# Batch norm and GELU with four slots for x, GELU ahead of the copies, and a quarter of the sums on TensorE

## The chip, the cores and the metric

The kernel runs on one NeuronCore of a Trainium2 chip. Five engines work side by side and meet only through semaphores: TensorE (PE, with its weight loads as PEld), VectorE (DVE), ScalarE (ACT), GpSimd (POOL) and SyncE (SP, which here issues DMAs). The metric is the device time of one execution in microseconds (us), smaller is better.

## The reference, cut to what matters

The input x is 8 images of 384 channels and 32 x 32 pixels, float32. The program computes

```
x = x + gelu(batch_norm(deform_conv(group_norm(x))))      # offsets and masks from two small convolutions
t = to_tokens(x)                                          # 8 x 1024 tokens of 384 channels
t = t + block_attention(layer_norm(t))
t = t + head_attention(layer_norm(t))
x = from_tokens(t)
```

The part around the change is the end of the first line. Batch norm needs mean and variance of each channel over all images, so it starts when the last convolution tile is done. `yn = (y - mean) * rsqrt(var + 1e-5) * gamma + beta`, then the exact GELU, then the sum with the input, the transposition from channels to tokens, and for each token mean and variance over its 384 channels, which the next layer norm uses.

## The kernel before, in words

The program is a row of blocks, and each block gives every engine its own instruction list. A barrier of all engines stands between two blocks. The first block makes the offsets and a table of corners, `deform_conv` gathers, mixes and multiplies (until 1567 us), `batch_norm_gelu` is the stage of this case (until 1671 us), `block_attention` and `head_attention` follow.

`batch_norm_gelu` works on halves of an image: a half is 4 tiles (GROUP) of 128 pixels, with 384 channels as 3 x 128 (CH). There are 16 halves, numbered 0 to 15 here. The tensor `y` holds the convolution's output of all images on chip, and later the tokens. In a turn on one half

- SP loads the half of x into `c_x` (L780, 768 KB). There are two slots, one for each half of an image, and a slot is loaded again when TensorE has transposed all of it (`transposed`);
- ACT applies scale, shift and GELU, one instruction for each of 3 channel blocks, into `c_act`, two slots (L860);
- POOL adds the two in place in `c_x` (L803), and a root for 4 tiles of the image before follows (L797, a power of -1/2 on 4 elements);
- TensorE transposes the sum, 12 transpositions for a half, three to a PSUM bank `c_tps`, four banks for a half (L895);
- ACT copies the first two banks into `y` (L872, `copies`), DVE copies the other two (L821) and takes their statistics (L822), then those of ACT's two from `y` (L829), and makes mean and variance of them (L832, L835, L836). `measured` and `copied` tell TensorE that the banks are free.

The order on each engine is written by hand. The first image's halves stand ahead of a loop on the chip (`Fori`) over the other seven images; ACT's loop runs GELU of a half, then the copies of the half before. DVE starts the stage with the statistics of batch norm (L844), for which it waits until `gamma` and `beta` have come (`consts`, L782 and L783, the first DMAs of the block).

In the listing below, `halves` is the helper that makes the first image and the loop.

Of the kernel before, what the change touches and what calls it, by code (L numbers as in the profile page):

```python
# [8 lines left out]
ACT = mybir.ActivationFunctionType  # L9
# [81 lines left out]
def build(nc, io):  # L91
# [6 lines left out]
    with ExitStack() as whole:  # L98
# [27 lines left out]
        with ExitStack() as layers:  # L126
            y = sb(layers, "y", [BLOCKS, CH, P])
            conv_stats = sb(layers, "conv_stats", [CH, GROUPS, 6])
            with ExitStack() as conv:
                tap_index = nc.dram_tensor("tap_index", (GROUPS, P, TAPS * GROUP), U32, kind="Internal").ap()  # L130
                corner_w = nc.dram_tensor("corner_w", (GROUPS, P, CORNERS * TAPS * GROUP), F32, kind="Internal").ap()
                w_conv = sb(conv, "b_w", [TAPS, CH, C])
                b_conv = sb(conv, "b_b", [CH])
                conv_consts = sem("conv_consts")
                offsets_and_table(nc, io, sem, sb, bank, x_img, table, ident, tap_index, corner_w, neg_half, y, w_conv,
                                  b_conv, conv_consts, shared)
                deform_conv(nc, io, sem, sb, bank, table, ident, tap_index, corner_w, y, conv_stats, w_conv, b_conv,
                            conv_consts, shared)
            with ExitStack() as blocks:
                w_qkv = sb(blocks, "d_w_qkv", [CH, 3 * C])  # L140
                w_proj = sb(blocks, "d_w_proj", [CH, C])
                rot_a = sb(blocks, "d_rot_a", [C])
                rot_b = sb(blocks, "d_rot_b", [C])
                w_ln = sb(blocks, "d_w_ln", [2, C])
                causal = sb(blocks, "d_causal", [P])
                block_consts = ((w_qkv, "w_qkv"), (w_proj, "w_proj"), (rot_a, "rot_cos"), (rot_b, "rot_sin"),
                                (w_ln, "w_ln"), (causal, "causal"))
                consts = sem("d_consts")
                batch_norm_gelu(nc, io, sem, sb, bank, x_img, ident, neg_half, y, conv_stats, token_stats, token_rstd,
                                block_consts, consts)  # L150
                block_attention(nc, io, sem, sb, bank, ident, neg_half, y, tokens, token_stats, token_rstd,
                                [tile for tile, _ in block_consts], consts, head_consts, b_quarters, head_loaded)
# [375 lines left out]
def deform_conv(nc, io, sem, sb, bank, table, ident, tap_index, corner_w, y, conv_stats, w_conv, b_conv, conv_consts, shared):  # L528
# [6 lines left out]
    with ExitStack() as mem:  # L535
# [21 lines left out]
        with nc.Block() as block:  # L557
            @block.sync
            def _(sp):
# [8 lines left out]
                for g in range(2):  # L568
                    load_places(0, g)
                with sp.Fori(0, BATCH - 1) as n:  # L570
# [159 lines left out]
def batch_norm_gelu(nc, io, sem, sb, bank, x_img, ident, neg_half, y, conv_stats, token_stats, token_rstd,  # L730
                    block_consts, block_loaded):

    WIDE = GROUP * P
    with ExitStack() as mem:
        x_in = [sb(mem, f"c_x{u}", [CH, WIDE]) for u in range(2)]
        act_out = [sb(mem, f"c_act{u}", [CH, WIDE]) for u in range(2)]
        gamma = sb(mem, "c_gamma", [CH])
        beta = sb(mem, "c_beta", [CH])
# [10 lines left out]
        consts = sem("c_consts")  # L749
        x_loaded = [sem(f"c_x_loaded{u}") for u in range(2)]  # L750
# [13 lines left out]
        LAST = BATCH - 1  # L764

        def halves(eng, turn):

            for u in range(2):
                turn(0, u, True)
            with eng.Fori(1, BATCH) as n:  # L770
                for u in range(2):
                    turn(n, u, False)

        with nc.Block() as block:
            @block.sync
            def _(sp):
                def turn(n, u, first):
                    if not first:
                        sp.wait_ge(transposed, GROUP * (2 * n + u - 1))
                    sp.dma_start(x_in[u][:], x_img[n, :, :, u * WIDE:(u + 1) * WIDE]).then_inc(x_loaded[u], 16)  # L780

                sp.dma_start(gamma[:], io["gamma"]).then_inc(consts, 16)  # L782
                sp.dma_start(beta[:], io["beta"]).then_inc(consts, 16)  # L783
                for u in range(2):
                    turn(0, u, True)
                for tile, name in block_consts:
                    sp.dma_start(tile[:], io[name]).then_inc(block_loaded, 16)
                with sp.Fori(1, BATCH) as n:
                    for u in range(2):
                        turn(n, u, False)  # L790

            @block.gpsimd
            def _(pool):
                def root(n, u):
                    group = bass.ds(TILES * n + GROUP * u, GROUP)
                    pool.wait_ge(token_var, 2 * n + u + 1)
                    nc.gpsimd.tensor_tensor(token_rstd[:, group], tvar[:, group], neg_half[:, 0:GROUP],  # L797
                                            ALU.pow).then_inc(token_done, 1)

                def turn(n, u, first):  # L800
                    pool.wait_ge(act_ready, 2 * n + u + 1)
                    pool.wait_ge(x_loaded[u], 16 * (n + 1))
                    nc.gpsimd.tensor_tensor(x_in[u][:], x_in[u][:], act_out[u][:], ALU.add).then_inc(summed, 1)  # L803
                    if not first:
                        root(n - 1, u)
# [3 lines left out]
                halves(pool, turn)  # L809
                for u in range(2):  # L810
                    root(LAST, u)

            @block.vector
            def _(dve):
                def turn(n, u, first):
                    c = Chain(dve, lchain, 3 * (2 * n + u))
                    for i in range(GROUP // 2, GROUP):
                        count = TILES * n + u * GROUP + i
                        dve.wait_ge(transposed, count + 1)
                        tile = tps[u * GROUP + i][:, 0:C]  # L820
                        nc.vector.tensor_copy(y[:, bass.ds(count, 1)].rearrange("p n o q -> p (n o q)"), tile)  # L821
                        last = nc.vector.bn_stats(tst[:, i], tile)  # L822
                    c.step(last)
                    dve.sem_inc(measured, 1)
                    dve.wait_ge(copied, 2 * n + u + 3)
                    dve.nop(nofuse=True)
                    for i in range(GROUP // 2):
                        tile = y[:, bass.ds(TILES * n + u * GROUP + i, 1)].rearrange("p n o q -> p (n o q)")
                        last = nc.vector.bn_stats(tst[:, i], tile)  # L829
# [4 lines left out]
                    group = bass.ds(TILES * n + u * GROUP, GROUP)  # L834
# [3 lines left out]
                dve.sem_inc(summed, 2)  # L838
                dve.sem_inc(measured, 2)
                dve.sem_inc(copied, 2)  # L840
                dve.wait_ge(consts, 32)
# [4 lines left out]
                nc.vector.tensor_scalar(var[:], mv[:, :, 1], 1e-5, None, ALU.add).then_inc(var_ready, 1)  # L846
                dve.wait_ge(rstd_ready, 1)
# [3 lines left out]
                halves(dve, turn)  # L851

            @block.scalar
            def _(act):
                def gelu(n, u):

                    act.wait_ge(summed, 2 * n + u + 1)
                    act.nop(nofuse=True)
                    for o in range(CH):
                        last = nc.scalar.activation(  # L860
                            act_out[u][:, o].rearrange("p (b q) -> p b q", q=P),
                            y[:, bass.ds(TILES * n + u * GROUP, GROUP), o], ACT.Gelu,
# [3 lines left out]
                def copies(n, u):  # L866

                    for i in range(GROUP // 2):
                        count = TILES * n + u * GROUP + i
                        act.wait_ge(transposed, count + 1)  # L870
                        act.nop(nofuse=True)
                        last = nc.scalar.activation(y[:, bass.ds(count, 1)].rearrange("p n o q -> p (n o q)"),  # L872
                                                    tps[u * GROUP + i][:, 0:C], ACT.Copy)
                    last.then_inc(copied, 1)

                act.wait_ge(coef_ready, 1)
                gelu(0, 0)
                gelu(0, 1)
                copies(0, 0)
                with act.Fori(1, BATCH) as n:  # L880
                    gelu(n, 0)
                    copies(n - 1, 1)
                    gelu(n, 1)
                    copies(n, 0)
                copies(LAST, 1)

            @block.tensor
            def _(pe):
                def turn(n, u, first):
                    pe.wait_ge(summed, 2 * n + u + 3)  # L890
                    pe.wait_ge(measured, 2 * n + u + 1)
                    pe.wait_ge(copied, 2 * n + u + 1)
                    for i in range(GROUP):
                        for o in range(CH):
                            last = nc.tensor.transpose(tps[u * GROUP + i][:, o * P:(o + 1) * P],  # L895
                                                       x_in[u][:, o, i * P:(i + 1) * P], ident[:])
                        last.then_inc(transposed, 1)

                halves(pe, turn)

# [1560 lines left out]
```

## Time and profile before

| | |
|---|---|
| median of 3 runs | 3674.73 us (3672.86 to 3677.05) |
| the profiled execution | 3672.31 us, of which the span from first to last instruction is 3670.5 us |
| the batch norm stage in it | about 1567 to 1671 us of the span |
| mean granted TensorE clock | 0.955 of full speed over the span |

Busy shares over the whole span (PE 91%, DVE 74%, ACT 61%, POOL 40%) average over all stages. The stage of this case is under 3% of the span, so it is read in windows of its own: what each engine does in one image, which wait ends last before it, and how long one turn of each engine takes where it does not wait.

### The profile page before, as it was taken

Reading aid. Unit: us, or ns where it says so; the run is one execution under the profiler, and the core shown is the slowest. Engines: PE = TensorE matmul, PEld = TensorE weight load, DVE = VectorE, ACT = ScalarE, POOL = GpSimd, SP = SyncE. Lnnn points to the kernel's source line nnn. Section 1 sums busy time; section 2 is a strip of 40 time slices with the busy share of each in tenths; the row PEclk is TensorE's granted clock in tenths of the full one; section 3 lists DMA queues with packets and bytes.
Section 4 is the critical chain, followed back from the end, with each engine's and each line's share of the span. In section 5 each row is a group of like instructions: output and inputs, shape, how many; then the busy total and the mean of one; then the engine's idle time right before and its main releaser. Section 6 shows DMA issues by size and latency. Waiting matters only on the chain. (4 is left out here: it accounts for less than half of the span.)

```text
span 3670.5 us, 62059 instructions
## 1 busy us (share of the span) xinstructions
PE 3327.3 (91%) x18046; PEld 1920.4 (52%) x18046; DVE 2721.3 (74%) x5169; ACT 2249.4 (61%) x5369; POOL 1453.6 (40%) x1544
## 2 busy tenths in 40 slices
PE   7969999999999999937999999977988889889897
PEld 3434444444444444436888888853444444444443
DVE  4468878888888888756888888855677776776765
ACT  3434444444444444455777777755977778787785
POOL 2134444444444444363222222221154454544635
PEclk9989999999999999968999999978999999999997
DMA  9999989888999899641000000011322232232221
GB/s 363 370 357 343 336 334 350 325 328 333 348 342 345 334 342 344 257 156 54 17 15 17 17 17 17 17 54 49 87 72 62 81 91 66 76 92 64 57 67 54
DMA packets 230540, 647.07 MB, mean 176 GB/s; under 512 B 31143, under 2 KB 127943, under 8 KB 229959
## 3 DMA queue, kind: packets, MB, share of 16 engines
q0 software_dynamic: 82944, 453.02, 32.9%
q1 hardware_dynamic: 147398, 191.91, 16.5%
q8 instruction: 64, 1.05, 0.1%
q14 instruction: 134, 1.09, 0.1%
HBM read 520.21 MB, written 79.18 MB: 163 GB/s over the span
## 5 line engine op out<-in xcount | busy, mean ns | idle before, releaser
L697 PE MATMUL b_acc<-b_sampled,b_w 128*128 128x512 f32 x2592 | 1210.7, 594 | 0.0
L632 DVE SCALAR_TENSOR_TENSOR b_mix<-shared,b_weight,b_mix 128x384 f32<-128x384 f32 x864 | 531.5, 621 | 139.7 <-ACT b_mix L655 83.3
L697 PEld LDWEIGHTS b_acc<-b_sampled,b_w 128*128 128x128 f32 x2592 | 449.2, 191 | 347.3 <-issue 347.3
L664 ACT ACTIVATE b_sampled<-b_tps 128x384 f32<-128x384 f32 x576 | 282.1, 490 | 567.7 <-PE b_tps L715 567.7
L1985 DVE TENSOR_REDUCE e_neg_top<-e_next 128x1 f32<-128x1024 f32 x384 | 469.5, 1223 | 191.8 <-PE e_next L2298 164.0
L632 DVE SCALAR_TENSOR_TENSOR b_mix<-b_got,b_weight,b_mix 128x384 f32<-128x384 f32 x864 | 530.6, 619 | 92.8 <-ACT b_mix L655 56.2
L2152 ACT ACTIVATE e_prob<-e_s 128x512 f32<-128x512 f32 x768 | 416.3, 598 | 128.0 <-PE e_s L2310 126.7
L2137 ACT ACTIVATE e_unused<-e_next,e_neg_top 128x1024 bf16<-128x1024 f32 x384 | 430.2, 1120 | 100.1 <-DVE e_neg_top L1985 100.1
L588 POOL DMA_INDIRECT shared<-corner_table,b_index x288 | 294.1, 1021 | 418.7 <-DVE b_mix L632 324.9
L588 POOL DMA_INDIRECT b_got<-corner_table,b_index x288 | 292.1, 1014 | 356.8 <-DVE b_mix L632 299.4
L715 PEld LDWEIGHTS b_tps<-ident,b_mix 128*128 128x128 f32 x1728 | 223.0, 142 | 370.7 <-issue 327.5
L1205 ACT ACTIVATE d_w_qkv<-d_back,d_neg_top 128x128 f32<-128x128 f32 x768 | 269.0, 389 | 136.0 <-DVE d_neg_top L1108 136.0
L715 PE MATMUL b_tps<-ident,b_mix 128*128 128x128 f32 x1728 | 287.3, 276 | 56.0 <-DVE b_mix L632 50.6
L2298 PE MATMUL e_next<-e_stack 96*128 96x512 f32 x768 | 299.4, 472 | 11.8 <-ACT e_unused L2137 6.9
L2310 PE MATMUL e_s<-e_stack 98*128 98x512 f32 x768 | 271.2, 425 | 6.1 <-ACT e_prob L2152 5.1
L655 ACT ACTIVATE b_mix<-shared,b_weight 128x384 f32<-128x384 f32 x288 | 177.2, 615 | 104.7 <-ACT b_sampled L664 54.6
L2324 PE MATMUL e_acc<-e_prob,e_v 128*32 128x512 f32 x1536 | 214.0, 630 | 7.1 <-DVE e_ctx L1999 5.8
L655 ACT ACTIVATE b_mix<-b_got,b_weight 128x384 f32<-128x384 f32 x288 | 177.1, 615 | 54.5 <-ACT b_sampled L664 51.0
L1035 POOL TENSOR_TENSOR d_rqk<-d_ms,neg_half 128x2 f32<-128x2 f32 x64 | 44.8, 700 | 411.8 <-DVE d_ms L1078 411.8
L2298 PEld LDWEIGHTS e_next<-e_stack 96*128 96x128 f32 x768 | 126.6, 196 | 145.4 <-issue 89.9
L2310 PEld LDWEIGHTS e_s<-e_stack 98*128 98x128 f32 x768 | 147.1, 196 | 67.8 <-ACT e_prob L2152 38.8
L1205 ACT ACTIVATION_READ_ACCUMULATOR d_w_qkv<-d_back,d_neg_top 128x1 f32 x768 | 176.2, 229 | 0.0
(225 smaller groups left out, 5362.7 us busy)
## 6 DMA issues: line engine op xcount, KB each, us to landing
corner_table<-y SPq DMA_DIRECT2D x32, 1536.0 KB, 14.8
e_stack<-e_high SPq DMA_DIRECT2D x384, 64.0 KB, 2.0
shared<-in_x SPq DMA_DIRECT2D x8, 1536.0 KB, 10.1
c_x<-in_x SPq DMA_DIRECT2D x16, 768.0 KB, 4.4
tokens<-y SPq DMA_DIRECT2D x64, 192.0 KB, 1.9
e_tok<-tokens SPq DMA_DIRECT2D x8, 1536.0 KB, 7.2
e_stack<-e_low SPq DMA_DIRECT2D x192, 64.0 KB, 2.0
shared<-tokens SPq DMA_DIRECT2D x8, 1536.0 KB, 7.3
```

Source lines behind the costliest of these rows:

```text
L588: nc.gpsimd.indirect_dma_start(out=got[t % SLOTS][:], out_offset=None, in_=table[:, :], in_offset=bass.IndirectOffsetOnAxis(ap=index[g][:, ...
L632: ins = nc.vector.scalar_tensor_tensor(dst[:], src[:, q * C:(q + 1) * C], weight[g][:, q, k, i:i + 1], dst[:], ALU.mult, ALU.add)
L655: nc.scalar.activation(mix[t % MIXES][:], got[t % SLOTS][:, 0:C], ACT.Copy, scale=weight[g][:, 0, k, i:i + 1]).then_inc(begun, 1)
L664: nc.scalar.activation(sampled[s % 2][:, :, i * P:(i + 1) * P], tps[t % 2][:, 0:C].rearrange("p (o q) -> p o q", q=P), ACT.Copy).then_inc( ...
L697: last = nc.tensor.matmul(acc[g][co][:], w_conv[:, k, ci, co * P:(co + 1) * P], sampled[s % 2][:, ci], start=(k == 0 and ci == 0), stop=(k ...
L715: last = nc.tensor.transpose(tps[t % 2][:, o * P:(o + 1) * P], mix[t % MIXES][:, o * P:(o + 1) * P], ident[:])
L1205: last = nc.scalar.activation(prob[:, head], b_s[r][:, c * P:(c + 1) * P], ACT.Exp, bias=neg_top[:, head:head + 1], scale=SCALE, accum_out ...
L1985: nc.vector.reduce_max(neg_top[s % 2][:, t:t + 1], b_next[t % 2][:], AX.X, negate=True).then_inc(top_ready, 1)
L2137: nc.scalar.activation(unused[t % 2][:], b_next[t % 2][:], ACT.Exp, bias=neg_top[s % 2][:, t:t + 1], accum_out=den[s % 2][:, t:t + 1]).the ...
L2152: nc.scalar.activation(prob[(2 * c + f) % 8][:], b_s[f][:], ACT.Exp).then_inc(prob_ready, 1)
L2298: last = nc.tensor.matmul(b_next[t % 2][:, f * HALF:(f + 1) * HALF], stack[k][0:96, 0, t * P:(t + 1) * P], stack[k][0:96, 1, f * HALF:(f + ...
L2310: nc.tensor.matmul(b_s[f][:], stack[k][0:98, 1, c * P:(c + 1) * P], stack[k][0:98, 0, f * HALF:(f + 1) * HALF], start=True, stop=True).the ...
```

## The change

In `batch_norm_gelu`:

- x has four slots in `shared` (memory that the convolution has used until then), one for each of four halves in a row, and a slot waits for the transpositions of four halves before. The six constants of the next block are loaded one by one behind the x loads of halves 4 to 9, where they stood ahead of the loop.
- `gamma` and `beta` are loaded at the start of `deform_conv`, and DVE waits for them only where it multiplies by gamma.
- ACT begins with a one-element GELU (`c_warm`). GELU of half h+2 stands ahead of the copies of half h; it waits for POOL's sum of h and for TensorE's first tile of h, both of which read the slot of `c_act`.
- POOL adds 3 of a half's 4 tiles. The last tile of the half goes first through TensorE: for each channel block a product of x with the identity and one of `c_act` with the identity, summed in PSUM, so 6 matmuls for that tile and 9 transpositions for the others.
- POOL's root is taken once an image, on 8 elements.
- All loops on the chip are written out, for 16 halves on each engine.

```
+            gamma = sb(layers, "c_gamma", [CH])
+            beta = sb(layers, "c_beta", [CH])
+            norm_loaded = sem("c_norm_loaded")
...
                 for g in range(2):
                     load_places(0, g)
+                sp.dma_start(gamma[:], io["gamma"]).then_inc(norm_loaded, 16)
+                sp.dma_start(beta[:], io["beta"]).then_inc(norm_loaded, 16)
...
-        x_in = [sb(mem, f"c_x{u}", [CH, WIDE]) for u in range(2)]
+        x_in = [shared[:, s].rearrange("p (o q) -> p o q", q=WIDE) for s in range(SLOTS)]
...
+        def tile_of(i):
+            return (i + GROUP - 1) % GROUP
...
+                def load_x(h):
+                    n, u = divmod(h, 2)
+                    if h >= SLOTS:
+                        sp.wait_ge(transposed, GROUP * (h - SLOTS + 1))
+                    sp.dma_start(x_in[h % SLOTS], x_img[n, :, :, u * WIDE:(u + 1) * WIDE]).then_inc(
+                        x_loaded[h % SLOTS], 16)
+                for h in range(SLOTS):
+                    load_x(h)
+                for h in range(SLOTS, HALVES):
+                    load_x(h)
+                    if h - SLOTS < len(block_consts):
+                        tile, name = block_consts[h - SLOTS]
+                        sp.dma_start(tile[:], io[name]).then_inc(block_loaded, 16)
...
+                for h in range(HALVES):
+                    pool.wait_ge(act_ready, h + 1)
+                    pool.wait_ge(x_loaded[h % SLOTS], 16 * (h // SLOTS + 1))
+                    x_part = x_in[h % SLOTS][:, :, 0:WIDE - P]
+                    nc.gpsimd.tensor_tensor(x_part, x_part, act_out[h % 2][:, :, 0:WIDE - P], ALU.add).then_inc(summed, 1)
+                    if h > 2 and h % 2:
+                        root(h // 2 - 1)
+                root(BATCH - 1)
...
-                dve.wait_ge(consts, 32)
                 c = Chain(dve, chain, 0)
...
+                dve.wait_ge(norm_loaded, 32)
                 dve.wait_ge(rstd_ready, 1)
...
+                nc.scalar.activation(warm[:], neg_half[:, 0:1], ACT.Gelu)
                 act.wait_ge(coef_ready, 1)
...
+                for h in range(2):
+                    gelu(h)
+                for h in range(HALVES):
+                    if h + 2 < HALVES:
+                        gelu(h + 2)
+                    copies(h)
...
+                for h in range(HALVES):
+                    slot = x_in[h % SLOTS]
+                    if h >= 2:
+                        pe.wait_ge(measured, h - 1)
+                        pe.wait_ge(copied, h - 1)
+                    pe.wait_ge(x_loaded[h % SLOTS], 16 * (h // SLOTS + 1))
+                    pe.wait_ge(act_ready, h + 1)
                     for i in range(GROUP):
+                        cols = slice(tile_of(i) * P, (tile_of(i) + 1) * P)
+                        if i == 1:
+                            pe.wait_ge(summed, h + 1)
                         for o in range(CH):
+                            out = tps[h % 2 * GROUP + i][:, o * P:(o + 1) * P]
+                            if i == 0:
+                                nc.tensor.matmul(out, slot[:, o, cols], ident[:], start=True, stop=False)
+                                last = nc.tensor.matmul(out, act_out[h % 2][:, o, cols], ident[:], start=False,
+                                                        stop=True)
+                            else:
+                                last = nc.tensor.transpose(out, slot[:, o, cols], ident[:])
                         last.then_inc(transposed, 1)
```

POOL's list before, from the first root-taking turn of the loop to the loop's end (`c_x` is the slot of x, `c_act` what GELU wrote, ISA and REGISTER_ALU rows keep the loop's counts):

```order
L803 TENSOR_TENSOR c_x<-c_x,c_act 128x1536 [waits c_x_loaded0]
L796 ISA
L797 ISA [waits c_token_var]
L797 TENSOR_TENSOR token_rstd<-c_tvar,neg_half 128x4
L801 REGISTER_ALU
L803 TENSOR_TENSOR c_x<-c_x,c_act 128x1536 [waits c_x_loaded1,c_act_ready]
L796 REGISTER_ALU
L797 ISA [waits c_token_var]
L797 TENSOR_TENSOR token_rstd<-c_tvar,neg_half 128x4
```

POOL's list now, from the third half on (`shared` is a slot of x):

```order
L806 TENSOR_TENSOR shared<-shared,c_act 128x3x384 [waits c_x_loaded2,c_act_ready]
L806 TENSOR_TENSOR shared<-shared,c_act 128x3x384 [waits c_x_loaded3,c_act_ready]
L797 TENSOR_TENSOR token_rstd<-c_tvar,neg_half 128x8 [waits c_token_var]
L806 TENSOR_TENSOR shared<-shared,c_act 128x3x384 [waits c_x_loaded0,c_act_ready]
L806 TENSOR_TENSOR shared<-shared,c_act 128x3x384 [waits c_x_loaded1,c_act_ready]
L797 TENSOR_TENSOR token_rstd<-c_tvar,neg_half 128x8 [waits c_token_var]
```

Two sums now stand between two roots, and a root stands ahead of every even half's sum from half 4 on.

TensorE's list before, in the loop, one half:

```order
L890 REGISTER_ALU
L891 REGISTER_ALU [waits c_summed]
L895 MATMUL c_tps<-ident,c_x 128x128 [waits c_copied,c_measured]
L895 MATMUL c_tps<-ident,c_x 128x128 x11
L770 REGISTER_ALU
L770 COMPARE_AND_BRANCH
```

TensorE's list now, one half:

```order
L896 MATMUL c_tps<-ident,shared 128x128 [waits c_x_loaded2,c_act_ready,c_copied,c_measured]
L897 MATMUL c_tps<-ident,c_act 128x128
L896 MATMUL c_tps<-ident,shared 128x128
L897 MATMUL c_tps<-ident,c_act 128x128
L896 MATMUL c_tps<-ident,shared 128x128
L897 MATMUL c_tps<-ident,c_act 128x128
L900 MATMUL c_tps<-ident,shared 128x128 [waits c_summed]
L900 MATMUL c_tps<-ident,shared 128x128 x8
```

The wait for POOL's sum has moved behind six matmuls, which wait for x and GELU alone.

## Rows read from the trace of the kernel before

**Rows 1.** Window, the stage: us, busy of PE, PEld, DVE, ACT, POOL; granted clock, DMA

```profile
1566.90:1670.60 103.70, 39.83 (x192) 34.47 (x192) 61.40 (x199) 51.04 (x81) 71.31 (x33) 0.63 0.46 153
```

**Rows 2.** Timeline, one image: start us, length us, engine, line, [idle <-releaser]

```profile
1599.76 3.43 POOL L803 TENSOR_TENSOR c_x<-c_x,c_act 128x1536 f32<-128x1536 f32 x1 [2.04 <-DMA c_x<-in_x]
1603.42 2.79 PE L895 MATMUL c_tps<-ident,c_x 128*128 128x128 f32 x12 [4.94 <-POOL c_x L803]
...
1606.39 4.74 SPq L780 DMA_DIRECT2D c_x<-in_x  x2
...
1610.77 3.44 POOL L803 TENSOR_TENSOR c_x<-c_x,c_act 128x1536 f32<-128x1536 f32 x1 [2.23 <-DMA c_x<-in_x]
```

**Rows 3.** Timeline, the stage's opening

```profile
1564.97 1.88 DVE L614 BATCH_NORM_STATS2 conv_stats<-y 128x6 f32<-128x512 f32 x3
1567.34 0.34 SPq L782 DMA_DIRECT2D c_gamma<-in_gamma  x1
...
1571.00 1.48 DVE L844 BATCH_NORM_AGGREGATE c_mv<-conv_stats 128x2 f32<-128x96 f32 x3 [4.15 <-DMA c_beta<-in_beta]
...
1574.35 1.28 ACT L860 ACT_TABLE_LOAD   x1 [21.41 <-DVE c_shift L850]
1575.65 4.33 ACT L860 ACTIVATE c_act<-y,c_shift,c_scale 128x512 f32<-128x512 f32 x6
```

**Rows 4.** DMA, the stage's first load of x: KB, us from issue to landing

```profile
c_x<-in_x SPq DMA_DIRECT2D x1, 768.0 KB, 4.7
```

**Rows 5.** Timeline of DVE: turn 0, written out, with no wait inside

```profile
1583.64 0.56 DVE L821 COPY y<-c_tps 128x384 f32<-128x384 f32 x1 [9.39 <-PE c_tps L895]
...
1587.36 0.17 DVE L835 COPY token_stats<-c_tmv 128x8 f32<-128x8 f32 x1
1587.44 0.16 DVE L836 TENSOR_SCALAR c_tvar<-c_tmv 128x4 f32<-128x4 f32 x1
1587.51 0.55 DVE L821 COPY y<-c_tps 128x384 f32<-128x384 f32 x1
```

**Rows 6.** Timeline, DVE's turn 1 and POOL beside it

```profile
1588.93 3.42 POOL L803 TENSOR_TENSOR c_x<-c_x,c_act 128x1536 f32<-128x1536 f32 x1 [4.16 <-DMA c_x<-in_x]
...
1590.79 0.38 DVE L832 BATCH_NORM_AGGREGATE c_tmv<-c_tst 128x2 f32<-128x6 f32 x4
1591.20 1.17 DVE L835 COPY token_stats<-c_tmv 128x8 f32<-128x8 f32 x1
```

**Rows 7.** Timeline, the last two turns

```profile
1660.76 0.56 DVE L821 COPY y<-c_tps 128x384 f32 x1 [2.46 <-PE c_tps L895]
...
1665.14 0.56 DVE L821 COPY y<-c_tps 128x384 f32 x1
...
1669.51 1.01 POOL L797 TENSOR_TENSOR token_rstd<-c_tvar,neg_half 128x4 f32<-128x4 f32 x1 [3.38 <-DVE c_tvar L836]
```

**Rows 8.** Groups of POOL, whole span: xcount | busy us, mean ns | idle before

```profile
L1042 POOL TENSOR_TENSOR d_qk<-d_part_a,d_part_b 128x384 f32<-128x384 f32 x128 | 128.1, 1001 | 110.5 <-DVE d_part_b L1093 110.2
...
L803 POOL TENSOR_TENSOR c_x<-c_x,c_act 128x1536 f32<-128x1536 f32 x16 | 54.9, 3430 | 21.5 <-DMA c_x<-in_x 17.2 <-ACT c_act L860 4.3
...
L1035 POOL TENSOR_TENSOR d_rqk<-d_ms,neg_half 128x2 f32<-128x2 f32 x64 | 44.8, 700 | 411.8 <-DVE d_ms L1078 411.8
...
L797 POOL TENSOR_TENSOR token_rstd<-c_tvar,neg_half 128x4 f32 x14 | 14.3, 1021 | 0.0
```

**Rows 9.** Groups of ACT in the stage

```profile
L860 ACT ACTIVATE c_act<-y,c_shift,c_scale 128x512 f32 x42 | 31.0, 804 | 0.4
L872 ACT ACTIVATE y<-c_tps 128x384 f32 x28 | 13.3, 490 | 33.3 <-PE c_tps L895 32.7
```

**Rows 10.** Timeline of TensorE: ordinary float32 products, of 128 and of 512 columns

```profile
2471.71 1.65 PE L2254 MATMUL e_z<-e_share,e_h_sum 128*128 128x128 f32 x6 [0.65 <-DVE e_h_t L1938]
...
1552.25 10.47 PE L697 MATMUL b_acc<-b_sampled,b_w 128*128 128x512 f32 x24
```

**Rows 11.** One line's view: DVE's copy to token_stats over the stage: ns min/median/max

```profile
L835 DVE COPY token_stats<-c_tmv x16: 170/172/1170, 1587.4 to 1669.1; 128x8 f32 x14, 128x8 f32<-128x8 f32 x2
```

More of the change, by code:

```diff
@@ L137, in build @@
                 deform_conv(nc, io, sem, sb, bank, table, ident, tap_index, corner_w, y, conv_stats, w_conv, b_conv,
-                            conv_consts, shared)
+                            conv_consts, shared, gamma, beta, norm_loaded)
             with ExitStack() as blocks:
@@ L149, in build @@
                 batch_norm_gelu(nc, io, sem, sb, bank, x_img, ident, neg_half, y, conv_stats, token_stats, token_rstd,
-                                block_consts, consts)
+                                block_consts, consts, shared, gamma, beta, norm_loaded)
                 block_attention(nc, io, sem, sb, bank, ident, neg_half, y, tokens, token_stats, token_rstd,
@@ L525, in _, with deform_conv @@
                 turn(BATCH // 2 - 1, 1)
-def deform_conv(nc, io, sem, sb, bank, table, ident, tap_index, corner_w, y, conv_stats, w_conv, b_conv, conv_consts, shared):
+def deform_conv(nc, io, sem, sb, bank, table, ident, tap_index, corner_w, y, conv_stats, w_conv, b_conv, conv_consts, shared,
+                gamma, beta, norm_loaded):
     STEPS = 2 * TAPS
@@ L730, in batch_norm_gelu @@
 def batch_norm_gelu(nc, io, sem, sb, bank, x_img, ident, neg_half, y, conv_stats, token_stats, token_rstd,
-                    block_consts, block_loaded):
+                    block_consts, block_loaded, shared, gamma, beta, norm_loaded):
     WIDE = GROUP * P
+    HALVES = 2 * BATCH
+    SLOTS = 4
     with ExitStack() as mem:
-        x_in = [sb(mem, f"c_x{u}", [CH, WIDE]) for u in range(2)]
+        x_in = [shared[:, s].rearrange("p (o q) -> p o q", q=WIDE) for s in range(SLOTS)]
         act_out = [sb(mem, f"c_act{u}", [CH, WIDE]) for u in range(2)]
-        gamma = sb(mem, "c_gamma", [CH])
-        beta = sb(mem, "c_beta", [CH])
+        warm = sb(mem, "c_warm", [1])
         mv = sb(mem, "c_mv", [CH, 2])
@@ L747, in batch_norm_gelu @@
         tps = [bank(mem, f"c_tps{i}") for i in range(2 * GROUP)]
-        consts = sem("c_consts")
-        x_loaded = [sem(f"c_x_loaded{u}") for u in range(2)]
+        x_loaded = [sem(f"c_x_loaded{s}") for s in range(SLOTS)]
         var_ready = sem("c_var_ready")
@@ L762, in batch_norm_gelu @@
         token_done = sem("c_token_done")
[L764 to L772, printed above, removed]
+        def tile_of(i):
+            return (i + GROUP - 1) % GROUP
         with nc.Block() as block:
@@ L776, in _ @@
             def _(sp):
[L777 to L790, printed above, removed]
+                def load_x(h):
[4 more added lines that the diff above has]
+                        x_loaded[h % SLOTS], 16)
@@ L792, in _, with root @@
+                for h in range(SLOTS):
[5 more added lines that the diff above has]
+                        sp.dma_start(tile[:], io[name]).then_inc(block_loaded, 16)
             @block.gpsimd
             def _(pool):
[L794 to L797, printed above, removed]
+                def root(n):
+                    group = slice(TILES * n, TILES * (n + 1))
+                    pool.wait_ge(token_var, 2 * (n + 1))
+                    nc.gpsimd.tensor_tensor(token_rstd[:, group], tvar[:, group], neg_half[:, 0:TILES],
@@ L798, in root @@
                                             ALU.pow).then_inc(token_done, 1)
[L800 to L805, printed above, removed]
                 pool.wait_ge(var_ready, 1)
                 nc.gpsimd.tensor_tensor(rstd[:], var[:], neg_half[:, 0:CH], ALU.pow).then_inc(rstd_ready, 1)
-                halves(pool, turn)
@@ L810, in _ @@
-                for u in range(2):
-                    root(LAST, u)
+                for h in range(HALVES):
[5 more added lines that the diff above has]
+                        root(h // 2 - 1)
@@ L813, in _, with tile @@
+                root(BATCH - 1)
             @block.vector
             def _(dve):
-                def turn(n, u, first):
-                    c = Chain(dve, lchain, 3 * (2 * n + u))
-                    for i in range(GROUP // 2, GROUP):
[L818 to L822, printed above, removed]
+                def tile(h, i):
+                    return tps[h % 2 * GROUP + i][:, 0:C]
@@ L823, in turn, with tokens_of @@
+                def tokens_of(h, i):
+                    return y[:, GROUP * h + tile_of(i)].rearrange("p o q -> p (o q)")
+                def turn(h):
+                    c = Chain(dve, lchain, 3 * h)
+                    for i in range(GROUP // 2, GROUP):
+                        dve.wait_ge(transposed, GROUP * h + i + 1)
+                        nc.vector.tensor_copy(tokens_of(h, i), tile(h, i))
+                        last = nc.vector.bn_stats(tst[:, tile_of(i)], tile(h, i))
                     c.step(last)
@@ L824, in turn @@
                     dve.sem_inc(measured, 1)
-                    dve.wait_ge(copied, 2 * n + u + 3)
-                    dve.nop(nofuse=True)
+                    dve.wait_ge(copied, h + 1)
                     for i in range(GROUP // 2):
-                        tile = y[:, bass.ds(TILES * n + u * GROUP + i, 1)].rearrange("p n o q -> p (n o q)")
-                        last = nc.vector.bn_stats(tst[:, i], tile)
+                        last = nc.vector.bn_stats(tst[:, tile_of(i)], tokens_of(h, i))
@@ L850, in _, with gelu @@
                 nc.vector.tensor_tensor(shift[:], beta[:], shift[:], ALU.subtract).then_inc(coef_ready, 1)
-                halves(dve, turn)
+                for h in range(HALVES):
+                    turn(h)
             @block.scalar
             def _(act):
-                def gelu(n, u):
-                    act.wait_ge(summed, 2 * n + u + 1)
-                    act.nop(nofuse=True)
+                def gelu(h):
+                    if h >= 2:
+                        act.wait_ge(summed, h - 1)
+                        act.wait_ge(transposed, GROUP * (h - 2) + 1)
@@ L864, in gelu, with copies @@
                     last.then_inc(act_ready, 1)
-                def copies(n, u):
+                def copies(h):
                     for i in range(GROUP // 2):
[L869 to L873, printed above, removed]
+                        act.wait_ge(transposed, GROUP * h + i + 1)
+                        last = nc.scalar.activation(y[:, GROUP * h + tile_of(i)].rearrange("p o q -> p (o q)"),
+                                                    tps[h % 2 * GROUP + i][:, 0:C], ACT.Copy)
@@ L887, in _ @@
+                for h in range(HALVES):
+                    if h + 2 < HALVES:
+                        gelu(h + 2)
+                    copies(h)
             @block.tensor
             def _(pe):
[L889 to L892, printed above, removed]
+                for h in range(HALVES):
+                    slot = x_in[h % SLOTS]
+                    if h >= 2:
+                        pe.wait_ge(measured, h - 1)
+                        pe.wait_ge(copied, h - 1)
+                    pe.wait_ge(x_loaded[h % SLOTS], 16 * (h // SLOTS + 1))
+                    pe.wait_ge(act_ready, h + 1)
```

21 lines of the change are left out of this document (3 added, 18 removed).

## The prediction, made before the changed kernel ran

> **What bounds the kernel now.** First the window of the stage [rows 1]: in 103.7 us POOL is busy for 71.3, DVE for 61.4, ACT for 51.0 and TensorE for 39.8. No engine is full, so a loop of waits sets the pace. Then the timeline of one image [rows 2], read backwards from a start of POOL: POOL's sum at 1610.77 had been idle for 2.23 us until a load of x landed; that load was issued at 1606.39; its issue waited until TensorE, which had begun at 1603.42, was through with the slot; and TensorE had waited for the POOL sum that began at 1599.76. So one slot goes round by sum 3.43, handoff 0.2, transpositions 2.8 and 0.2, issue and load 4.4: 11.0 us an image. Two slots take turns, so a half costs about 5.4 us. The same number comes out at DVE: its last turn begins at 1665.14 [rows 7], its first at 1583.64 [rows 5], 81.5 us for 15 turns, 5.43 each. A DVE turn that waits for nothing lasts 3.87 us (1583.64 to 1587.51, [rows 5]). That is the room in the steady part.
>
> The opening [rows 3] is a chain too. DVE ended the convolution at 1566.85 (1564.97 + 1.88), the block is open by 1567.34, but DVE sits 4.15 us until beta has landed; later ACT loads its GELU table for 1.28 us with everyone waiting.
>
> **The change part by part.** All sums are against the profiled execution, 3672.31 us, which lies 2.42 us under the median of the runs shown, 3674.73.
>
> *Opening.* With gamma and beta loaded earlier, DVE starts at about 1567.3 instead of 1571.00, 3.7 us earlier. The two loads move into the opening of the convolution on SP's queue, behind the first places and ahead of SP's loop, which there waits for a whole half of mixes; some 0.8 us of issue (0.34 us for one, [rows 3]) are hidden by that wait. The table load now stands before ACT's wait, beside DVE's statistics, and costs nothing; without that cover it would cost its 1.28 us again. From DVE's first instruction to ACT's start took 1574.35 - 1571.00 = 3.35 us, so GELU starts at 1570.65 and half 0 is through at 1572.8 (six in 4.33 us, [rows 3]). x is issued first, at 1567.34, and lands 4.7 us later [rows 4], at 1572.0: in time. POOL's sum of 3 tiles takes 1152 elements instead of 1536. The rows give 1.00 us for 384 and 3.43 for 1536 [rows 8], so 2.11 ns an element and 2.62 us for 1152; its bounds are 2.57 (three quarters) and 3.43 (rows with gaps cost as much as the whole). Sum 0 ends at 1575.5. Beside it TensorE does the six identity products. An ordinary float32 product of this size is in the trace: six of them in 1.65 us at the low clock [rows 10], so they are done before the sum. Six transpositions follow, 0.233 each (12 in 2.79, [rows 2]), 1.4 us, and with handoffs of 0.2 DVE's turn 0 starts at 1577.3, against 1583.64: **6.3 us gained**.
>
> *Steady part.* With four slots a load is issued when the half four turns back is transposed, and has two turns or more to land where it needs 4.4 us: the wait for x goes. The constants behind it put one larger load (w_qkv) in front of x of half 5, once, and the two or three turns of lead cover that; uncovered it would cost a few us once. What is late next? ACT needs 3 x 0.80 + 2 x 0.49 = 3.4 us a half [rows 9]. TensorE at the low clock needs 1.65 + 9 x 0.233 = 3.75. POOL needs 2.62 and half a root. Four elements take 1.02 us and two 0.70 [rows 8], so 0.16 for each further one and 1.66 for eight (bounds: 1.02, no dearer than now; 2.04, two of the present ones): 3.45 a half. DVE needs 3.87 and is the bound. Written out, each DVE turn looks like turn 0 of now; the looped ones took 4.38 (1660.76 to 1665.14, [rows 7]) with the loop's register instructions in them. So 15 turns gain 15 x (5.43 - 3.87) = **23.4 us**. ACT's GELU ahead of the copies keeps `copied` early enough: the copies of a half follow its GELU by two halves, while DVE comes to them 2.2 us into its turn.
>
> *What DVE meets.* In turn 1 of now [rows 6] DVE's small copy (L835) starts at 1591.20 and takes 1.17 us instead of 0.17, and ends where POOL's sum ends (1588.93 + 3.42 = 1592.35); the aggregation just before it ran through the same sum at its usual 0.38. So a copy that falls into a sum waits for the sum's end. The Trainium skill (SBUF — State Buffer, Who interferes with whom) has this as a rule: a VectorE copy in a two-port mode and a GpSimd instruction exclude each other, whoever starts second waits for the whole of the first. The trace agrees, in that one copy.
>
> In the new order it will happen regularly. A root waits for both turns of its image. The second one's variance is out as DVE's next turn begins, so the root starts 0.2 us into that turn and ends at 1.86, the next sum runs from there to 4.5, and the copy stands at 3.72 (1587.36 - 1583.64, [rows 5]): 0.8 us late. The second sum after the root, 4.5 to 7.2, falls between two copies. Six sums follow a root directly (halves 4, 6, ..., 14): 6 x 0.8 = **4.8 us lost**. The bounds are 0 and, with a whole sum of 2.62 in each of 16 turns, 41.9; I take the phase worked out here.
>
> *Tail.* From the start of the last turn to the end of the last root: before, 1669.51 + 1.01 - 1665.14 = 5.38; now 3.87 + 0.2 + 1.66 = 5.7: **0.3 lost**.
>
> Sum: 6.3 + 23.4 - 4.8 - 0.3 = 24.6 us. The following blocks issue what they did; their constants land long before. 3672.31 - 24.6 = 3647.7, and as a median 3674.73 - 24.6 = 3650.1. TensorE's clock (0.63 in the stage, half speed for much of it, [rows 1]) doesn't decide, since even at 1.2 GHz its turn is under DVE's.
>
> **The rivals.**
>
> 1. *The copies miss the sums.* If the root takes nearer 1.0 us or the phase drifts, nothing is lost to the collisions: 29.4 gained, 3645.3. For it: only one of 16 copies was long (median 172 ns, longest 1170, [rows 11]). Against: the root ties POOL's phase to DVE's turns.
> 2. *POOL or DVE less quick than hoped.* If the sum still takes 3.43, the collision is 0.2 + 1.66 + 3.43 - 3.72 = 1.6 instead of 0.8 six times, and the first sum ends 0.8 later: 5.4 less. If DVE's turn stays at 4.38, 15 x 0.5 = 7.6 are gone, but collisions shrink by about 0.5 each: 4.6 less. Either way some 20 gained, 3655. For it: the sum's rows now have gaps, and all looped turns were slow. Against: the two written-out turns were quick.
> 3. *TensorE becomes the bound.* If an identity product costs what one of 512 columns costs (24 in 10.47 us, 0.44 each, [rows 10]), a half takes 2.6 + 2.1 and 0.2 of handoff, 4.9 us; the forecast's mean turn is 3.87 + 4.8/15 = 4.19, so 15 x 0.7 = 10.6 less: 3660.7. Against: the six products in 1.65 us.
> 4. *The wait for x stays*, because the four loads and the constants queue behind one another: only opening and tail remain, 6.0 gained, 3668.7. Against: 4.4 us of load against two turns of lead.
> 5. *Slower: DVE's copy waits for a whole sum in every turn.* The place is L835. The gain without collisions is 29.4 us over 16 turns, so from 1.84 us a turn on the kernel is slower; at 2.62 it is 41.9 - 29.4 = 12.5 slower, 3687. For it: the long copy of rows 6. Against: DVE would have to run in step with each sum, and there are two sums and a root between two roots.
> 6. *Slower: an ordinary product is several times a transposition.* At four times 0.233 a half takes 5.6 + 2.1 + 0.2 = 7.9 us on TensorE, 15 x (7.9 - 4.19) = 55.7 more than forecast: 3705.8. The Trainium skill (TensorE: Matmul & The Clock Gate, Terms) gives a transpose mode that is 4 times faster for FP32, which would make it so. Against: in rows 10 an ordinary product of the same size is no dearer than a transposition.
>
> **How the numbers follow.** Forecast 0.50, rival 1 0.17, rival 2 0.17, rival 3 0.07, rival 4 0.04, rival 5 0.03, rival 6 0.02. Predicted: 3650. The range takes in the first four with some room on both sides: 3643 to 3662. About 0.2% (7.3 us) is what a measurement of this kernel can tell from no change: faster by more, the forecast and rivals 1 to 3, 0.91; within, rival 4, 0.04; slower, rivals 5 and 6, 0.05.
>
> **What would show it.** In the new profile: the stage's last root ends near 1646 instead of 1670.5. DVE's first turn starts near 1577.3. POOL's idle time behind loads of x, 17.2 us now [rows 8], is gone or a few us. DVE's turns show 3.87 and about 4.7 us in alternation, with L835 at some 1 us in six of 16. The sum takes 2.62 and the root 1.66. Six identity products take 1.65 us or less. I am wrong in the steps if DVE waits at its copies from PSUM for TensorE turn after turn (then a chain through POOL or ACT sets the pace), if DVE has gaps that nothing releases, or if the later blocks differ by more than 2 us.

## The result, and the profile after

The changed kernel takes 3648.47 us (median of 6 runs, 3641.89 to 3655.70) against 3675.82 us (6 runs, 3672.86 to 3677.05): a ratio of 0.9926, interval 0.9913 to 0.9940, 27.4 us less. The forecast was 24.6 us less, 3650.

The stage is counted here from the end of the convolution's last statistics to the end of the last root. Before, that is 1566.85 to 1670.52 [rows 3, 7], 103.7 us. The timeline of the changed kernel's opening answers to rows 3 (start us, length us, engine, line, [idle <-releaser]):

```profile
1570.40 1.88 DVE L620 BATCH_NORM_STATS2 conv_stats<-y 128x6 f32<-128x512 f32 x3
1572.77 10.72 SPq L781 DMA_DIRECT2D shared<-in_x  x5
1572.77 1.28 ACT L871 ACT_TABLE_LOAD   x1 [14.40 <-PEq L561]
1572.81 1.48 DVE L840 BATCH_NORM_AGGREGATE c_mv<-conv_stats 128x2 f32<-128x96 f32 x3 [0.53 <-PEq L561]
...
1576.17 4.34 ACT L858 ACTIVATE c_act<-y,c_shift,c_scale 128x512 f32<-128x512 f32 x6 [1.90 <-DVE c_shift L847]
1578.48 5.20 POOL L806 TENSOR_TENSOR shared<-shared,c_act 128x1152 f32<-128x1152 f32 x2 [3.01 <-ACT c_act L858]
1578.54 0.77 PE L896 MATMUL c_tps<-ident,shared 128*128 128x128 f32 x2 [10.39 <-ACT c_act L858]
...
1581.23 1.86 PE L900 MATMUL c_tps<-ident,shared 128*128 128x128 f32 x9
...
1582.76 0.56 DVE L823 COPY y<-c_tps 128x384 f32<-128x384 f32 x1 [6.62 <-PE c_tps L900]
...
1647.35 1.64 POOL L797 TENSOR_TENSOR token_rstd<-c_tvar,neg_half 128x8 f32<-128x8 f32 x1 [5.93 <-DVE c_tvar L836]
```

The convolution ended at 1572.28 here, the last root at 1648.99: the stage is 76.7 us, **27.0 less**. DVE's idle time at L840 is 0.53 us where it was 4.15 at L844, and the table load lies beside it. DVE's turn 0 starts 10.5 us after the convolution, where it was 16.8.

The steady part, POOL and DVE over two turns, answers to rows 5 and 6:

```profile
1606.77 0.55 DVE L823 COPY y<-c_tps 128x384 f32<-128x384 f32 x1
1606.94 1.65 POOL L797 TENSOR_TENSOR token_rstd<-c_tvar,neg_half 128x8 f32<-128x8 f32 x1 [1.38 <-DVE c_tvar L836]
...
1608.56 5.21 POOL L806 TENSOR_TENSOR shared<-shared,c_act 128x1152 f32<-128x1152 f32 x2
...
1610.41 0.79 DVE L835 COPY token_stats<-c_tmv 128x8 f32<-128x8 f32 x1
1611.12 0.16 DVE L836 TENSOR_SCALAR c_tvar<-c_tmv 128x4 f32<-128x4 f32 x1
1611.19 0.55 DVE L823 COPY y<-c_tps 128x384 f32<-128x384 f32 x1
...
1614.82 0.17 DVE L835 COPY token_stats<-c_tmv 128x8 f32<-128x8 f32 x1
...
1614.97 0.55 DVE L823 COPY y<-c_tps 128x384 f32<-128x384 f32 x1
```

After its first turn DVE never waits for TensorE any more. A root starts as the turn begins (1606.94), two sums follow, and the copy at 1610.41 ends with the first of them (1610.41 + 0.79 = 1611.20, and 1608.56 + 2.61 = 1611.17). So turns of 4.42 and 3.78 us alternate; there are six of the long ones.

The groups that answer to rows 8 and 10 (xcount | busy us, mean ns | idle before):

```profile
L806 POOL TENSOR_TENSOR shared<-shared,c_act 128x1152 f32<-128x1152 f32 x16 | 41.7, 2625 | 3.5 <-ACT c_act L858 3.5
...
L896 PE MATMUL c_tps<-ident,shared 128*128 128x128 f32 x96 | 20.8, 299 | 23.4 <-DVEq L826 13.0 <-ACT c_act L858 10.4
L900 PE MATMUL c_tps<-ident,shared 128*128 128x128 f32 x144 | 19.4, 282 | 4.8 <-POOL shared L806 4.8
...
L797 POOL TENSOR_TENSOR token_rstd<-c_tvar,neg_half 128x8 f32<-128x8 f32 x8 | 13.2, 1646 | 15.3 <-DVE c_tvar L836 15.3
```

POOL's wait for loads of x, 17.2 us before, is gone. Read the counts too: 16 halves with 3 channel blocks make 48 products of x with the identity, but L896 has 96 matmul instructions.

The windows of the opening and of the steady part (us, busy of PE, PEld, DVE, ACT, POOL, then granted clock, DMA) answer to rows 1; the first line is the steady part before:

```profile
1583.60:1665.10 81.50, 37.13 (x182) 32.17 (x182) 55.61 (x180) 44.39 (x72) 62.77 (x29) 0.67 0.43 135
...
1572.30:1582.80 10.50, 4.26 (x20) 4.29 (x21) 2.18 (x8) 7.08 (x10) 5.21 (x3) 0.51 0.85 297
1582.80:1643.40 60.60, 39.89 (x318) 35.42 (x316) 55.91 (x181) 42.04 (x73) 48.75 (x22) 1.00 0.60 210
```

DVE is busy for 55.9 of 60.6 us, the waits of the late copies counted as busy, and waits for no other engine there, so it is the bound. TensorE runs at the full clock from the steady part's start, where the steady part before had 0.67.

### The profile page after: what moved, and what is told of

Read it like the earlier page. It is cut to its first block and busy times, and to the rows that moved or that the text cites. A ratio compares the mean times of both kernels' runs of the same rounds, so it can differ in the third digit from the quotient of the medians.

```text
span 3649.7 us, 61842 instructions
## 1 busy us (share of the span) xinstructions
PE 3328.9 (91%) x18190; PEld 1921.1 (53%) x18190; DVE 2723.8 (75%) x5169; ACT 2248.0 (62%) x5370; POOL 1435.3 (39%) x1536
```

## The experiments

The times of one kernel spread by 3 to 14 us, as much as some edits are worth, so the verdict of each rests on the stage in its profile, with the time beside it.

**Does the round of x set the pace, or do the loops?** First the kernel before with its loops written out (`for n in range(1, BATCH)` for each `Fori` of the stage).

> The kernel before with its batch norm loops written out and nothing else. The stage is counted from the end of the convolution's last statistics to the end of the last root: 103.7 us before, 76.7 us after. Theory (the round of a slot of x, 11.0 us an image, sets the pace): DVE's turns get shorter but wait longer, stage 101 to 104, time as before. Rival (register instructions and jumps of the loops set the pace): 15 x 0.5 = 7.6 less, stage 96, some 8 us faster.

Measured: stage 102.2 us, ratio 0.9995 (0.9985 to 1.0004), no difference. The theory holds. POOL's group in it:

```profile
L803 POOL TENSOR_TENSOR c_x<-c_x,c_act 128x1536 f32<-128x1536 f32 x16 | 54.8, 3427 | 20.4 <-DMA c_x<-in_x 16.0 <-ACT c_act L860 4.3
```

The wait for x is still 16.0 us: shorter DVE turns only made DVE wait longer. Then four slots on top of it:

```
-        x_in = [sb(mem, f"c_x{u}", [CH, WIDE]) for u in range(2)]
+        x_in = [shared[:, s].rearrange("p (o q) -> p o q", q=WIDE) for s in range(4)]
...
-                        sp.wait_ge(transposed, GROUP * (2 * n + u - 1))
+                        sp.wait_ge(transposed, GROUP * (2 * n + u - 3))
```

> The written-out kernel before with four slots for x and nothing else of the change. Theory: no wait of POOL for x is left; POOL's own work, 2 x 3.43 + 2 x 1.02 = 8.9 us an image, is next, so 7 images gain some 2 us each: stage about 90, 10 to 15 us faster than before. Rival (another chain has the same length as the loads, so the wait only changes its name): stage 101 to 104.

Measured: stage 91.2 us, ratio 0.9956 (0.9939 to 0.9972). Against the written-out loops the slots alone are worth 11.0 us, and the wait for x is gone. What is left is POOL and DVE in step:

```profile
L805 POOL TENSOR_TENSOR shared<-shared,c_act 128x1536 f32<-128x1536 f32 x16 | 55.0, 3442 | 5.3 <-ACT c_act L862 5.3
...
L837 DVE COPY token_stats<-c_tmv 128x8 f32<-128x8 f32 x16 | 14.0, 876 | 0.6
```

DVE's small copy now takes 876 ns on average where 172 is its own time. With a root behind every sum it is late in 14 of 16 turns, most by 0.75 us: the mechanism of the prediction's rival 5, at part of a sum instead of a whole one.

**Are four slots needed with the shorter sum?** The changed kernel with `SLOTS = 2`.

> The changed kernel with two slots for x instead of four. Theory: a slot's round is 2.6 (sum) + 0.2 + 1.2 to 2.1 (transpositions) + 0.1 + 4.4 (load) + 0.1 = 8.6 to 9.5 us an image against the 8.2 that DVE and its late copies take, and the second image's loads begin later: stage 80 to 87 against 76.7. Rival (with the shorter sum two slots do): 77.

Measured: stage 83.5 us, ratio 0.9945 (0.9928 to 0.9962). POOL waits for x again:

```profile
L806 POOL TENSOR_TENSOR shared<-shared,c_act 128x1152 f32<-128x1152 f32 x16 | 41.9, 2621 | 20.0 <-DMA shared<-in_x 17.0 <-ACT c_act L858 3.0
```

**What does TensorE's tile bring?** The changed kernel with POOL summing all four tiles and TensorE transposing all four.

```
-                    x_part = x_in[h % SLOTS][:, :, 0:WIDE - P]
+                    x_all = x_in[h % SLOTS]
...
-                            if i == 0:
-                                nc.tensor.matmul(out, slot[:, o, cols], ident[:], start=True, stop=False)
...
+                            last = nc.tensor.transpose(out, slot[:, o, cols], ident[:])
```

> The changed kernel with all four tiles of a half summed on POOL and 12 transpositions, as before. Theory (the sum after each root runs over DVE's small copy): root and sum end 0.2 + 1.65 + 3.43 = 5.3 us into DVE's turn instead of 4.5, the copy stands at 3.65, so six copies are 1.6 us late instead of 0.63, and the first sum ends 0.8 later: stage 83 to 84. Rival (DVE is the bound and POOL is off its path): 77.

Measured: stage 83.7 us, ratio 0.9943 (0.9926 to 0.9960). From its timeline, one late turn:

```profile
1606.87 1.65 POOL L797 TENSOR_TENSOR token_rstd<-c_tvar,neg_half 128x8 f32<-128x8 f32 x1 [0.56 <-DVE c_tvar L836]
...
1608.49 6.83 POOL L806 TENSOR_TENSOR shared<-shared,c_act 128x1536 f32<-128x1536 f32 x2
1610.34 1.60 DVE L835 COPY token_stats<-c_tmv 128x8 f32<-128x8 f32 x1
```

The same chain with a longer sum: the copy ends at 1611.94, with the first sum (1608.49 + 3.42 = 1611.91). Turns alternate between 5.22 and 3.79. The copy is 1.43 us late here, not the expected 1.6. TensorE's tile is worth 7.0 us: 6 x 0.80 in these turns, 1.5 in the opening and 0.7 in turn 0. POOL was not full, since it still idles 0.56 us ahead of this root: the sum's length sets how late the copy is.

**Do the late copies cost what they seem to?** DVE's small copy and small tensor_scalar are taken away.

```
-                        last = nc.vector.bn_aggr(tmv[:, i], tst[:, i])
+                        last = nc.vector.bn_aggr(token_stats[:, GROUP * h + i], tst[:, i])
...
+                    nc.gpsimd.tensor_scalar(tvar[:, group], token_stats[:, group, 1], 1e-5, None, ALU.add).then_inc(eps_done, 1)
```

> The changed kernel, but DVE's aggregation writes mean and variance straight into token_stats, and POOL adds the 1e-5 ahead of its root, so that DVE has no small copy and no small tensor_scalar left. Theory (these are what POOL's sums hold up, 3.8 us in six turns, and they take 0.16 us a turn themselves): no turn is late, turns of about 3.65, stage 70 to 73 against 76.7, 4 to 6 us faster than the changed kernel. Rival (a late copy costs nothing, since another chain through POOL, ACT and TensorE has the same pace): 16 x 0.16 = 2.6 less at most, stage 74 to 77, with the late turns still there in another row.

Measured: stage 72.9 us, 3.8 less; time 3646.05, ratio to before 0.9923 (0.9909 to 0.9936). In its timeline of DVE, one turn:

```profile
1595.34 0.56 DVE L826 COPY y<-c_tps 128x384 f32<-128x384 f32 x1
...
1597.45 1.02 DVE L832 BATCH_NORM_STATS2 c_tst<-y 128x6 f32<-128x384 f32 x2
1598.58 0.38 DVE L835 BATCH_NORM_AGGREGATE token_stats<-c_tst 128x2 f32<-128x6 f32 x4
1599.11 0.56 DVE L826 COPY y<-c_tps 128x384 f32<-128x384 f32 x1
```

All turns but one (4.11) are 3.76: no aggregation waits, though POOL's sums run beside them. The theory holds for the late turns; the 0.16 us of the two instructions came back only as 0.03, since a gap of 0.15 us after the aggregation took their place.

**Was it the early load of gamma and beta, or the place of the wait?** Both loads go back to the head of the stage's SP list, the wait stays ahead of the multiplication by gamma.

> The changed kernel with the loads of gamma and beta back at the opening of the stage, ahead of x, and DVE's wait for them where the change put it. Theory (the wait's place did it: beta lands 3.6 us after the opening and is needed 2.8 us after it): GELU 0.9 us later, stage 77.6 against 76.7. Rival (the early load did it): the 4.15 us of before come back, stage 80 to 81.

Measured: stage 76.8 us, time 3648.09, GELU 3.9 us after the convolution as in the changed kernel. From its timeline:

```profile
1571.70 0.34 SPq L782 DMA_DIRECT2D c_gamma<-in_gamma  x1
1572.09 0.43 SPq L783 DMA_DIRECT2D c_beta<-in_beta  x1
...
1574.52 0.16 DVE L845 TENSOR_TENSOR c_scale<-c_rstd,c_gamma 128x3 f32<-128x3 f32 x1 [1.08 <-POOL c_rstd L801]
```

L845 waits for POOL's root, not for a load: beta landed 1.7 us after its issue, at about 1573.8, where it took 3.2 before. The place of the wait did all of it in this run; the 0.9 us that I expected to lose did not come. With a landing as slow as before, L845 would have waited some 0.8 us (an estimate, 1572.09 + 3.2 against 1574.52), so the early loads can still be worth that much.

**Does the order of GELU and copies matter?** `copies(h)` ahead of `gelu(h + 2)` on ACT.

> The changed kernel with ACT's old order: copies of half h, then GELU of half h+2. Theory (DVE and its late copies set the pace, and a sum of POOL starts 2 us or more after its GELU is done): GELU comes some 1.2 us later and nobody waits for it, stage 77 against 76.7. Rival (the order of GELU and copies is what the change gains in the steady part besides slots and sums): 1.2 us a half, stage 85 or more.

Measured: stage 77.6 us, time 3649.35. The 0.9 us lie in the first turn (4.68 instead of 3.80, its copy falls into a sum); from the second turn on the turns are the same 3.79 and 4.42. GELU ahead of the copies brings next to nothing here.

**How much do executions differ by themselves?** The changed kernel once more.

> The changed kernel once more, for the spread between executions: its six times run from 3641.9 to 3655.7 us, those of before from 3672.9 to 3677.1. In the profiles so far the convolution ended at 1566.85 us before and at 1572.28 after. Theory (the convolution's pauses at image boundaries are chance): the stage again 76.7 within 0.5, the convolution's end anywhere between 1563 and 1575. Rival (the change slows the convolution): its end again at 1572 or later, and earlier in the run with gamma and beta loaded late.

Measured: stage 76.65 us, time 3646.46 (3640.08 to 3650.72), the convolution's end at 1566.0. The theory holds. Over the twelve profiles of this case the convolution ended between 1562.4 and 1572.3; from the end of one half's statistics in the convolution to the next took 82.8 to 83.0 us in all of them inside one pass of its loop, and 83.2 to 87.7 in the six places where the loop goes on to the next image. What makes these pauses vary stays open.

**What is next?** Two further steps on the kernel without small copies. First DVE's aggregation of a half behind the next half's copies.

> As the kernel with the 1e-5 added on POOL (stage 72.9, DVE turns of 3.76), and DVE's aggregation moved one turn on, behind the next half's copies, so that no instruction of a DVE turn waits for the one before it. Theory: a DVE turn needs 1.95 + 0.38 + 1.02 + 0.15 = 3.5 us, but POOL needs 2 x 2.63 + 0.24 + 1.67 + 0.2 = 7.4 an image, 3.7 a half, and is the bound: stage 71.5 to 73. Rival (DVE's own turn is the bound): turns of 3.5, stage 68.5 to 70.

Measured: stage 74.3 us, time 3650.05. A miss for both: worse than 72.9. DVE's turns are 3.0 to 5.6 us. POOL's roots and sums stand in one list, and the statistics that a root waits for now come in the next turn:

```profile
PE c_tps L907 <- POOL shared L809: 13.1, 6, 3.4
DVE y L834 <- PE c_tps L907: 8.9, 6, 2.5
ACT c_act L865 <- POOL shared L809: 8.8, 5, 2.4
POOL c_tvar L798 <- DVE token_stats L825: 6.2, 6, 1.5
```

(The view of waits over 45 us: who <- for whom: us in total, times, longest.) POOL waits 6.2 us for the late statistics, and ACT, TensorE and DVE wait in turn for sums that stand behind. TensorE's granted clock was 0.92 in this window; what that adds was not separated. Then TensorE sums two tiles of each half on top of it:

```
-            return (i + GROUP - 1) % GROUP
+            return (i + GROUP - 2) % GROUP
...
-                            if i == 0:
+                            if i < 2:
```

> As the kernel with late aggregation, and TensorE sums two tiles of a half, POOL two. POOL then needs 2 x 1.81 + 2.1 = 5.7 us an image. TensorE needs 12 x 0.22 + 6 x 0.125 = 3.4 us a half at the full clock (12 x 0.43 + 6 x 0.233 = 6.6 at half the clock, in the opening). Theory (POOL was the bound): turns of 3.5 to 3.6, opening 1 to 2 us later, stage 70 to 71.5. Rival (TensorE becomes the bound, with its clock at half speed in some stretches): turns over 4, stage over 75.

Measured: stage 69.4 us, time 3645.00 (3638.34 to 3645.94), ratio 0.9909 (0.9892 to 0.9925): the shortest stage, 0.6 below the expected range. Turn 0 starts 12.3 us after the convolution (10.5 in the changed kernel), and turns are 3.2 to 3.6.

```profile
1585.00:1630.00 45.00, 44.74 (x395) 43.78 (x394) 41.43 (x133) 37.77 (x66) 34.69 (x25) 1.00 0.73 255
```

TensorE is now busy all the time, at the full clock, and is the bound, as the rival had it but without its long turns: its own work is 12 x 0.22 + 6 x 0.125 = 3.4 us a half. The medians of this version and of the changed kernel (3648.47 and 3646.46) lie as near to each other as single runs do, so the 7.3 us are read from the stage; the intervals to before overlap.

A shorter stage is not yet a faster kernel. From the last root to the end, the profile of this version took 2007.3 us and that of the version without small copies 2009.0, against 2000.7 and 2001.4 in the two of the changed kernel and 1997.1 to 2003.4 in the other eight. So in these two profiles what the stage gained on the changed kernel was lost behind it, wholly or nearly. Whether that is chance or follows from the shorter stage stays open.

## Why the prediction was right, and where it was not

| | forecast | measured |
|---|---|---|
| convolution's end to DVE's turn 0 | 10.45 | 10.48 |
| 15 turns | 15 x 3.87 + 4.8 = 62.9 | 60.6 |
| last turn and last root | 5.7 | 5.6 |
| stage | 79.1 | 76.7 |

*The bound* was named rightly. The slots' round set the pace: written-out loops alone moved the stage by 1.5 us, four slots by 11.0, and with two slots the wait came back in the changed kernel. The rest of the 27.0 is 4.9 in the opening, 7.0 for TensorE's tile, and 2.6 that no run separates: it holds the roots once an image, since GELU's place brought next to nothing. The shares hold for this order of steps; taken away from the changed kernel, two of the four slots cost nearly 7 us.

*The opening* came out to 0.1 us, but one of its terms gave nothing in the run that tried it: the early loads, as the late ones showed. The place of the wait and the earlier table load account for it (4.15 - 0.53 + 1.28 = 4.9 us, GELU at 8.8 and at 3.9 us after the convolution).

*The late copies* came as worked out, behind the six sums that were named, by the mechanism of the one copy in rows 6. Each cost 0.63 us instead of 0.8, and most of the difference is a slip in the sum: 0.8 is the time from the copy's start (3.72 into the turn) to the end of POOL's sum (4.5), but the copy's own 0.17 lies in it and is no loss, so the prediction's rows give 0.6. The 1.6 of rival 2, expected again of the kernel with all sums on POOL, has the same slip; 1.43 was measured. The page of the Trainium skill weighed there (SBUF — State Buffer, Who interferes with whom) agrees with the ends of these copies and sums: each of the six copies ended 0.03 us after its sum. Taking the copies away gave the time back, which makes this the best shown of the steps.

*DVE's turn* is 3.79 instead of 3.87, and the 0.08 lie in the gap ahead of the statistics from `y` (0.22 us at L829 before, 0.14 now; an idle instruction stood there before, which no run tried apart). That is 15 x 0.08 = 1.2 of the 2.3 us that the 15 turns differ by; six collisions of 0.63 instead of 0.8 are 1.0.

*One price was read wrongly*, and with it the sentence that TensorE's clock does not decide. The six instructions in rows 10 are three products: an ordinary float32 product is two matmul instructions. The tile's six products took 2.7 us in the opening (1578.54 to 1581.23, at 0.51), not 1.65, and were done 0.1 us after the sum (1578.48 + 2.60) instead of well before it. At that clock a half would need 2.7 + 2.1 = 4.8 us, more than DVE's 3.79, which is rival 3. It did not come about because the granted clock was 1.00 in the steady part, with TensorE busy for 39.9 of 60.6 us; without the tile's products it was 0.73 (all sums on POOL, 1580 to 1640). The prediction had not counted on that, so it was right here by luck. A whole steady part at the low clock was not tried. One half ran at it with GELU behind the copies (clock 0.50 from 1637 to 1640): its six products took 2.5 us, and DVE's turns stayed as they were, so a single half is covered. In the steady part, three products of x and three of `c_act` in turn, then the nine transpositions:

```profile
1585.25 0.39 PE L896 MATMUL c_tps<-ident,shared 128*128 128x128 f32 x2
1585.47 0.39 PE L897 MATMUL c_tps<-ident,c_act 128*128 128x128 f32 x2
...
1586.59 1.16 PE L900 MATMUL c_tps<-ident,shared 128*128 128x128 f32 x9
```

One product follows the other by 0.22 us, a transposition by about 0.125, so a product costs less than twice as much and rival 6 did not come. The Trainium skill (TensorE: Matmul & The Clock Gate, Terms) speaks of a transpose mode that is 4 times faster for FP32; the measurement decides.

*The whole* is nearer than its parts warrant: the medians differ by 27.4, the stage by 27.0, the forecast said 24.6. The time came out within 2 us of 3650 partly by luck, since the forecast was taken off a median of 3674.73 and all six runs before give 3675.82. In the one profiled pair the spans differ by only 20.8, since the convolution happened to end 5.4 us later (27.0 - 5.4 = 21.6, and the later blocks took 0.8 more).

## What to carry to other kernels

Read a slow steady part backwards from one buffer's start, write down its round, and compare it with each engine's turn without waits: the difference is what more slots give, and the next engine's turn is where it stops. Then lay the new phases side by side and look for small VectorE copies inside long GpSimd instructions, because a copy of 0.17 us can cost a sum's remainder each time it falls into one. Before pricing an instruction by a row, compare the row's count with the loops of its source line, since one call can be two instructions.

## What was not expected of the hardware

An ordinary 128 x 128 float32 product is issued as two matmul instructions (96 for 48), 0.43 us at the low and 0.22 us at the full clock, against 0.233 and 0.125 for a transposition. The change that made TensorE busier also brought its granted clock in the steady part from 0.67 to 1.00; without the tile's products on TensorE it was 0.73. A 1.5 KB load took 3.2 us in one kernel and 1.7 in another, with the same engine, queue and order ahead of it.
